# Which of two tanh activations ScalarE issues first in a scan of 512 dependent stages

## The reference, cut to what matters

```python
def _derivative(q, p, drive, coupling, bias):
    i_couple = jnp.tanh(q) @ coupling.T
    dq = q - q ** 3 / 3.0 - p + drive + i_couple + bias
    dp = EPSILON * (q + ALPHA - BETA * p)
    return (dq, dp)
...
(_, _), q_trace_tbn = jax.lax.scan(scan_fn, (q0, p0), drive_tbn)
...
gu = jnp.einsum('th,ehi->eti', x, We_gate_up)
h = _silu_and_mul(gu, I_MOE)
eo = jnp.einsum('eti,eih->eth', h, We_down)
```

## Time and profile before

| | |
|---|---|
| median of 3 runs | 664.38 us (664.13 to 665.31) |
| time of the profiled execution | 664.56 us |
| its span, first to last instruction | 662.6 us |
| busy: PE, PEld, DVE, ACT, POOL | 639.3, 609.1, 619.2, 359.5, 194.5 us |
| mean granted TensorE clock | 0.979 of full speed |

### The profile page before, as it was taken

How to read it: one execution, slowest core, us unless ns; L and a number is a source line. 1 busy time by engine, 2 the same in 40 slices (tenths; PEclk the granted TensorE clock), 3 DMA queues, 4 the chain that set the end, 5 groups by cost and what they waited for, 6 DMA issues and landing times.

```text
span 662.6 us, 33930 instructions
## 1 busy us (share of the span) xinstructions
PE 639.3 (96%) x12847; PEld 609.1 (92%) x12847; DVE 619.2 (93%) x4542; ACT 359.5 (54%) x1860; POOL 194.5 (29%) x436
## 2 busy tenths in 40 slices
PE   3789999999999999999999999999999999999998
PEld 2578899999999999999999999999999999999997
DVE  6899999999999999999999999999999999999951
ACT  2756555646555554655555465555556555555643
POOL 0001123242322324232332423233342323334244
PEclk9975799999999999999999999999999999999999
DMA  8800000000000000000000000000000000000000
GB/s 301 270 2 2 3 3 3 12 3 12 2 12 3 3 12 3 11 3 12 2 3 12 3 11 4 11 3 3 12 3 12 3 12 2 4 12 2 12 2 17
DMA packets 8628, 13.65 MB, mean 21 GB/s; under 512 B 1521, under 2 KB 7985, under 8 KB 8209
## 3 DMA queue, kind: packets, MB, share of 16 engines
q1 hardware_dynamic: 8464, 11.50, 5.3%
HBM read 9.40 MB, written 2.10 MB: 17 GB/s over the span
## 4 chain that ended last, share of the span: by engine, by line
PE 90%; DVE 7%; ACT 2%; issue 1%; DMA 0%; POOL 0%; DVEq 0%; SPq 0%
PE up_ps L561 28%; PE down_ps L576 21%; PE coup_ps L503 15%; PE coup_ps L509 13%; PE coup_ps L492 5%; PE coup_ps L496 3%; PE route_ps L541 2%; DVE w L701 2%; ACT hidden L368 1%; PE route_ps L522 1%; DVE q L777 1%; DVE th_lo L749 0%; DVE force L760 0%; DVE square_ps L746 0%; DVE square_ps L742 0%
## 5 line engine op out<-in xcount | busy, mean ns | idle before, releaser
L561 PE MATMUL up_ps<-q_hi,w 128*128 128x128 f16 x2176 | 238.3, 220 | 0.2 <-POOL q_lo L855 0.2
L892 POOL TENSOR_TENSOR hidden<-hidden,comb_s 128x128 f32<-128x128 f32 x272 | 123.3, 456 | 296.8 <-ACT th_hi L390 289.5
L390 ACT ACTIVATE th_hi<-q 128x32 f16<-128x32 f32 x384 | 88.0, 229 | 223.1 <-DVE q L777 222.2
L561 PE MATMUL up_ps<-q_lo,w 128*128 128x128 f16 x1088 | 201.3, 220 | 0.0
L503 PE MATMUL coup_ps<-th_hi,c 128*128 128x16 f16 x4096 | 181.1, 170 | 1.5 <-ACT th_hi L390 0.8
L576 PE MATMUL down_ps<-hidden,wd 128*128 128x128 f32 x1088 | 180.8, 290 | 0.0
L561 PEld LDWEIGHTS up_ps<-q_hi,w 128*128 128x128 f16 x2176 | 177.4, 98 | 0.7 <-POOL q_lo L855 0.4
L503 PEld LDWEIGHTS coup_ps<-th_hi,c 128*128 128x128 f16 x4096 | 139.1, 96 | 6.8 <-ACT th_hi L390 2.2
L576 PEld LDWEIGHTS down_ps<-hidden,wd 128*128 128x128 f32 x1088 | 141.8, 191 | 0.0
L509 PE MATMUL coup_ps<-th_lo,c 128*128 128x16 f16 x2048 | 131.2, 172 | 1.6 <-DVE th_lo L749 1.5
L431 ACT ACTIVATE act_s<-up_ps,unscale 128x128 f32<-128x128 f32 x272 | 99.2, 365 | 14.5 <-PE up_ps L561 10.5
(11 more groups left out here) (95 smaller groups left out, 1079.3 us busy)
## 6 DMA issues: line engine op xcount, KB each, us to landing
wf<-in_w_up SPq DMA_DIRECT2D x1, 4224.0 KB, 13.5
wd<-in_w_down SPq DMA_DIRECT2D x1, 2048.0 KB, 23.3
out<-out_s SPq DMA_DIRECT2D x16, 128.0 KB, 2.2
xs<-in_x SPq DMA_DIRECT2D x1, 1920.0 KB, 19.7
sel<-in_spread SPq DMA_DIRECT2D x1, 408.0 KB, 19.2
cf<-in_coupling SPq DMA_DIRECT2D x1, 256.0 KB, 2.6
xs<-in_x SPq DMA_DIRECT2D x1, 128.0 KB, 2.3
ident<-in_identity SPq DMA_DIRECT2D x1, 64.0 KB, 2.4
```

The lines of the kernel that those rows point to most:

```text
L390: nc.scalar.activation(th_hi[:], q[:], ACT.Tanh).then_inc(hi_ready, 1)
L561: last = nc.tensor.matmul(up_ps[(f * TILES + j) % UPS][:, h * TOK:(h + 1) * TOK], w16[:, part, k, h, j * P:(j + 1) * P], q[:, k, :], start ...
L892: nc.gpsimd.tensor_tensor(hidden[:, j, :], hidden[:, j, :], comb_s[:, j, :], ALU.mult).then_inc(weighed, 1)
```

## The change

ScalarE issues the fp32 tanh first and the f16 tanh second. The fp32 tanh raises no semaphore any more; `tanh_ready` is gone, and VectorE's `th_lo` waits for `hi_ready`, which the second activation raises. TensorE and GpSimd wait for `hi_ready` as before.

```diff
-        tanh_ready = sem("tanh_ready")
...
+                nc.scalar.activation(th, q[:], ACT.Tanh)
                 nc.scalar.activation(th_hi[:], q[:], ACT.Tanh).then_inc(hi_ready, 1)
-                nc.scalar.activation(th, q[:], ACT.Tanh).then_inc(tanh_ready, 1)
...
-                dve.wait_ge(tanh_ready, n + 1)
+                dve.wait_ge(hi_ready, n + 1)
                 nc.vector.tensor_tensor(th_lo[:], th, th_hi[:], ALU.subtract).then_inc(lo_ready, 1)
```

## The result

The changed kernel takes 677.36 us (median of 4 runs, 677.29 to 677.45) against 664.39 us (664.13 to 665.31, 4 runs). The ratio is 1.0193, with a 95% interval of 1.018 to 1.0205: 13.0 us slower. The forecast was 676.4 us, which is 12.0 us more than before. The profiled execution took 677.45 us, with a span of 675.5 us against 662.6.

A forecast was written before the change was run, and what follows sets the result against it. The prediction took a loop of latencies through both tanhs, th_lo, TensorE and q as the bound. Terms of 10.5, 0.5 and 1.0 us made 12.0 us more, 676.4 us; own range 674 to 679, 8-in-10 range 668.8 to 684.5.

The forecast's parts named there:

- The loop and the pair: Loop of q, both tanhs, th_lo and TensorE sets the pace; reordered tanh pair 0.03 us longer per loop stage, 10.5 us.
- The restart of 0.017 us: On ScalarE, 0.017 us after a wait falls on whichever tanh is first, giving 0.137 us between the two.
- The Trainium skill's 42 ns: Estimate from the skill's access overheads: tanh pair 42 ns longer with the SBUF write last, near the upper bound.
- The later start of TensorE: TensorE's th_hi matmuls wait 0.12 us longer for hi_ready, hidden behind VectorE's subtraction, which stays last by 0.03.
- the seven TensorE stages: Seven of 32 stages a block, where TensorE is last, pay 0.005 us each, 0.5 us in blocks 2 to 15.
- That work is queued behind `th_lo`, so a later `th_lo` moves it too.: VectorE's additional work in some stages was claimed to move with th_lo, so those stages were costed at 0.03 us too.
- the prediction's check: Stage pace before the change: 25 stages at 1.18 and 7 at 1.21 give 1.187 us, against 1.197 measured.
- I cost it at nothing.: GpSimd's q_lo and the up matmuls come 0.12 us later, under 0.5 us in all, or 1.4 without margin.
- The sum: 10.5 us for loop stages, 0.5 for TensorE stages and 1.0 for blocks 0 and 1, together 12.0 us.
- Blocks 0 and 1: Of 64 stages, partly paced by half-clocked TensorE or ScalarE's long instructions, half pay 0.03 us each, 1.0 us.
- The clock: Rival: TensorE falls to half clock more often, 1.5 us a stretch, 681 us for three; more than two added, 8%.
- No rival: Longer tail, 684 us, 10%; pair 0.012 longer, 669, 8%; no change, 664.4, 5%; clock falls, 8%; faster, 2%.

## Why the prediction came out, and where it didn't

*The loop and the pair.* Right, to the hundredth. The restart of 0.017 us was put ahead of whichever tanh is first: the fp32 row is 201 ns as the first and was 183 as the second, 18 ns. The distance between the two stayed at 0.13 to 0.14 and the second is 213 ns. The 18 ordinary loop stages pay 27 to 33 ns.

The Trainium skill's 42 ns (Perfetto Trace Analysis, "Optimizing Scalar/DVE Operations") has the right sign. The trace shows 213 - 183 = 30 ns between a second row to SBUF and one to PSUM, and the measured number is the one that the stages pay.

*The later start of TensorE.* Right, shown by the run that delays TensorE alone and by the rows of the changed kernel. In the seven TensorE stages the forecast had 5 ns; six of them pay 0.2 us in 14 blocks, where it was 0.4.

*VectorE's stages.* The step that failed reads: "That work is queued behind `th_lo`, so a later `th_lo` moves it too." In the first of every four stages the end of that work moves by a third of `th_lo`'s 30 ns. Line 753, the cubic term behind `th_lo`, waits for ScalarE's square. That comes behind both tanhs, 0.12 after the second one's start, in either order. Stage 8, before and after:

```profile
338.01 0.23 ACT L390 ACTIVATE th_hi<-q_raw 128x32 f16<-128x32 f32 x1 [0.39 <-DVE q_raw L777]
...
338.27 0.18 ACT L397 ACTIVATE square_ps<-q_trace 128x32 f32<-128x32 f32 x1
...
338.48 0.20 DVE L753 SCALAR_TENSOR_TENSOR square_ps<-square_ps,q_trace 128x32 f32<-128x32 f32 x1
...
338.94 0.25 DVE L777 SCALAR_TENSOR_TENSOR q<-coup_ps,c_un,force 128x32 f32<-128x32 f32 x1
```

```profile
344.21 0.20 ACT L389 ACTIVATE th_ps<-q_raw 128x32 f32<-128x32 f32 x1 [0.42 <-DVE q_raw L776]
...
344.47 0.18 ACT L396 ACTIVATE square_ps<-q_trace 128x32 f32<-128x32 f32 x1
...
344.70 0.19 DVE L752 SCALAR_TENSOR_TENSOR square_ps<-square_ps,q_trace 128x32 f32<-128x32 f32 x1
...
345.15 0.25 DVE L776 SCALAR_TENSOR_TENSOR q<-coup_ps,c_un,force 128x32 f32<-128x32 f32 x1
```

The square starts 0.26 us after ScalarE's start in both. Before, line 753 starts 0.03 behind the square's end (338.45), so it was the square that released it, and not `th_lo` ahead of it in the queue; it starts 0.47 after ScalarE's start, and line 752 in the changed kernel 0.49. The `q` that ends the chain starts 0.93 and 0.94 after it. The chain that ends last in these stages goes through the cubic term and `force`, and the square released it, with `th_lo` only just ahead of the square. So a later `th_lo` is hidden in part: by the averages over blocks 2 to 15, `th_lo` starts 30 ns later in stage 0, the cubic term 23 ns later, and its row is 190 ns where it was 200, so that `force` and `q` come 12 ns later. That the row is shorter because it no longer waits is likely, as with ScalarE's restart, but no run isolates it. The term was 2.5 us in the sum and is 0.8 us. The numbers before could have warned of it: these six stages were 1.21 to 1.23 us long and not 1.18, and they make most of the gap between 1.187 and 1.197 that the prediction's check left. The run with the new order in these stages alone shows the small cost by itself, and the one with the extra tanh, which moves the square, shows the full one.

*GpSimd.* The other step that failed: "I cost it at nothing." The prediction followed GpSimd's later start only to the one who waits for it by semaphore, the up matmuls behind `q_lo` (14 ns extra in stage 3, 0.2 us). It didn't look at what else runs while GpSimd's rows run. In stage 11 that is 2.9 us, as the two runs that move GpSimd's row away from `rest4` show.

*The sum.* The two misses are -1.7 and +2.8 us and nearly cancel. That 12.0 and 13.0 are so close is luck: 7.6 of the 13 us, the 18 ordinary stages, came as they were worked out. Blocks 0 and 1 gave 0.7 where 1.0 was put. The clock stayed as it was: granted 0.982 over the span against 0.979, with the same slices low, a little less so the earlier trace rows. No rival came true: the second row is 213 ns and not 229 or 183, and the first has its restart.

None of the runs points to a version that beats the kernel before.

## What to carry to other kernels

Where the next step waits for two small ScalarE instructions, put the one that writes SBUF first and the one that writes PSUM last, since only the last one's tail is on the path; here that is 30 ns a stage. Sum such a change stage by stage, and ask for every kind of stage which chain arrives last, since a delay in the second-last chain is partly free. And when an engine's start moves by a tenth of a microsecond, look at what runs beside it and not only at who waits for it: a GpSimd row can hold up a VectorE row with two SBUF inputs that no semaphore ties to it, here for 2.9 of 13 us.

## What of the hardware was unexpected

A VectorE instruction of 0.18 us that starts 0.03 us behind a GpSimd row of 0.45 us takes 0.46 us. With 0.18 us of GpSimd's row left to run the same instruction takes 0.22 us. With `th_lo` reading two SBUF tiles, such a row came up in 18 of 32 stages, in a kernel that was 77 us slower.

An instruction with one SBUF input can be held up too. `p_now` of line 774 (773), a TENSOR_SCALAR, takes 0.17 us with no GpSimd row beside it. In stages 23, 27 and 31 it runs beside GpSimd's row of line 892 (891). Stage 23 of one block, before and after:

```profile
356.25 0.45 POOL L892 TENSOR_TENSOR hidden<-hidden,comb_s 128x128 f32<-128x128 f32 x1 [0.73 <-ACT th_hi L390]
356.52 0.22 DVE L774 TENSOR_SCALAR p_now<-p_sum 128x32 f32<-128x32 f32 x1
```

```profile
363.06 0.46 POOL L891 TENSOR_TENSOR hidden<-hidden,comb_s 128x128 f32<-128x128 f32 x1 [0.76 <-ACT th_hi L390]
363.22 0.34 DVE L773 TENSOR_SCALAR p_now<-p_sum 128x32 f32<-128x32 f32 x1
```

It ends 0.04 us behind GpSimd's row both times, so it grows by 0.11 us when GpSimd starts later. This is where 4.6 us of VectorE's added rows come from. It costs nothing: the three stages pay 30 to 33 ns like their neighbours.

But not every GpSimd row does this. In the kernel with the fp32 tanh in SBUF, stage 9:

```profile
376.49 0.44 POOL L871 TENSOR_SCALAR first<-iota_s,which_f,prob 128x8 f32<-128x8 f32 x1 [2.24 <-ACT th_hi L392]
...
376.54 0.19 DVE L751 TENSOR_TENSOR th_lo<-th_s,th_hi 128x32 f16<-128x32 f32 x1
```

GpSimd's row has 8 columns here and lasts as long as the one of 128 columns in stage 11, and `th_lo` is not held up. Yet in the run with GpSimd later, line 664 was 0.05 us longer beside rows of this kind. Whether the columns, the kind of instruction or the place within GpSimd's row make the difference stays open.

On ScalarE a tanh row that follows directly on another is 16 to 18 ns shorter than one that starts after a wait, whichever memory it writes: 213 against 229 ns to SBUF, 183 against 201 ns to PSUM.
